# Two-layer attention and expert block: attention and queries on column halves of the array, maxima from high parts on row halves

## The reference

```python
q_hk = (hidden_q @ Wq.T).reshape(Bv, Sv, H, K)            # 16 heads, K = 128
q_big = einsum('bshk,hkq->bshq', q_hk, w_kc_q)            # q = 192
q_big = apply_rope(q_big, sin_q, cos_q)
kv_r = apply_rope(kv_c, sin_k, cos_k)                     # 1444 keys of 64
q_r = einsum('bshq,hqr->bhsr', q_big, W_qr)
k_r = einsum('bld,hdr->bhlr', kv_r, W_kr)
scores = einsum('bhsr,bhlr->bhsl', q_r, k_r)
attn = softmax(scores, axis=-1)
ctx_c = einsum('bhsl,bld->bhsd', attn, kv_r)
ctx_lat = einsum('bhsd,hkd->bhsk', ctx_c, w_kc_kv)
out = ctx @ Wo.T
```

## Time and profile before

| | |
|---|---|
| median of three runs | 2293.81 us |
| profiled execution, its own time | 2283.25 us |
| its span, first to last instruction | 2281.4 us |
| mean granted TensorE clock | 0.905 |
| TensorE matmul (PE) busy | 1857.9 us, 81% |
| VectorE (DVE) busy | 1492.1 us, 65% |
| ScalarE (ACT) busy | 1220.5 us, 53% |
| GpSimd (POOL) busy | 1117.1 us, 49% |

### The profile page before, as it was taken

The page is one execution under the profiler, slowest core; times in us unless marked ns, Lnnn a source line. Parts: engine busy times, 40 slices in busy tenths (PEclk is TensorE's granted clock), DMA queues, the critical chain, the costliest instruction groups (busy, mean ns, idle before and its releaser), DMA issues. The chain is left out here.

```text
span 2281.4 us, 38538 instructions
## 1 busy us (share of the span) xinstructions
PE 1857.9 (81%) x10550; PEld 1632.6 (72%) x10550; DVE 1492.1 (65%) x2799; ACT 1220.5 (53%) x2996; POOL 1117.1 (49%) x961
## 2 busy tenths in 40 slices
PE   4999958999999999999999973499993689837870
PEld 3677736888888888888888963499993466626870
DVE  4677777777777777767776433377774466656763
ACT  2111115777777767767777851366661266515650
POOL 0455528888788888878888852300004100014005
PEclk9999967999999999999999985699996599958985
DMA  5522251111111111111110002455542100026654
GB/s 159 197 58 57 55 176 55 63 63 63 45 54 63 64 31 63 63 64 63 63 54 11 16 8 78 140 197 196 204 165 58 34 1 0 0 77 196 198 164 113
DMA packets 115748, 195.76 MB, mean 86 GB/s; under 512 B 48213, under 2 KB 94265, under 8 KB 110161
## 3 DMA queue, kind: packets, MB, share of 16 engines
q1 hardware_dynamic: 107409, 180.88, 24.6%
q0 software_dynamic: 8192, 13.15, 2.0%
HBM read 147.01 MB, written 46.63 MB: 85 GB/s over the span
## 5 line engine op out<-in xcount | busy, mean ns | idle before, releaser
L501 POOL TENSOR_TENSOR EL<-E,EH 128x400 fp32r<-128x400 f32 x688 | 833.4, 1239 | 158.5 <-ACT EH L733 154.0
L599 DVE TENSOR_REDUCE PM<-bank 128x1 f32<-128x482 f32 (+1 forms) x624 | 397.2, 650 | 185.9 <-PE bank L578 182.9
L742 ACT ACTIVATE E<-bank 128x400 f32<-128x400 f32 x768 | 386.4, 503 | 212.8 <-PE bank L793 153.2
L733 ACT ACTIVATE EH<-E 128x400 fp32r<-128x400 f32 x768 | 407.0, 532 | 0.0
L175 PE MATMUL bank<-EH,KVH 128*128 128x400 f32 x768 | 283.1, 369 | 19.8 <-POOL EL L501 18.5
L578 PE MATMUL bank<-KH,QS 128*128 128x482 f32 (+1 forms) x624 | 250.9, 414 | 53.9 <-DVE KVL L549 27.6
L1248 POOL DMA_INDIRECT m_back<-rows_out,m_slots x64 | 64.8, 1013 | 450.8 <-DMA rows_out<-m_ys 421.2
L792 PE MATMUL bank<-QS,KH 128*128 128x400 f32 x768 | 272.1, 354 | 14.9 <-issue 9.1
L793 PE MATMUL bank<-QB,KB 66*128 66x400 f32 x768 | 269.1, 350 | 0.0
L175 PE MATMUL bank<-EH,KVL 128*128 128x400 f32 x768 | 265.7, 346 | 0.0
L175 PE MATMUL bank<-EL,KVH 128*128 128x400 f32 x768 | 265.5, 346 | 0.0
(11 more groups left out here) (244 smaller groups left out, 3983.3 us busy)
## 6 DMA issues: line engine op xcount, KB each, us to landing
m_stage_u<-in_m_up SPq DMA_DIRECT2D x20, 1392.0 KB
raw<-in_ctx_T SPq DMA_DIRECT2D x16, 1444.0 KB, 6.1
m_xg<-rows_in SPq DMA_DIRECT2D x55, 256.0 KB, 4.1
rows_out<-m_ys SPq DMA_DIRECT2D x55, 256.0 KB, 3.7
m_stage_d<-in_m_down SPq DMA_DIRECT2D x20, 696.0 KB
queries<-q_out SPq DMA_DIRECT2D x64, 200.0 KB, 2.4
QS<-queries SPq DMA_DIRECT2D x16, 800.0 KB, 6.1
rows_in<-zeros SPq DMA_DIRECT2D x5, 1792.0 KB
```

The source lines that it names most:

```text
L501: ops.tensor_tensor(EL[:, n % PB, :], E[:, n % EB, :], as_f32(EH[:, n % PB, :]), ALU.subtract).then_inc(sem, 1)
L599: nc.vector.tensor_reduce(PM[:, f:f + 1], psum[F0 + f % f_banks(b)][:, 0:KW[f % KC]], AX.X, ALU.max).then_inc(red_done, 1)
L733: nc.scalar.activation(EH[:, n % PB, :], E[:, n % EB, :], ACT.Copy).then_inc(hi_done, 1)
L742: nc.scalar.activation(E[:, n % EB, :], psum[S0 + n % SB][:, 0:CH], ACT.Exp).then_inc(exp_done, 1)
```

## The change

**Folding.** The 64 latent columns of `M2` are made once, not twice.

**Queries.** `narrow` works on a pair of heads: head 2j gives output rows 0 to 63, head 2j+1 rows 64 to 127 of one bank, four fp32 products of 64 columns of weights. The copy and the subtraction cover both heads at once, and SP stores a pair by four DMAs of 64 rows.

**Attention.** A step covers eight heads, so there are 24. `scores` has four products, even heads in one bank and odd heads in the next, with 128 rows in both kinds; one exponential of 2 x 400 columns reads both banks. `values` is two plain fp32 products, `KV` against the exponentials themselves, even heads to output rows 0 to 63 and odd heads to 64 to 127 of one bank; no high and low parts are made. The sums over keys are formed apart: VectorE sums the even heads' exponentials four key tiles at a time (`sum_even`), GpSimd adds the odd heads' tile by tile (`sum_odd`), and `sums` makes the sum over the 128 rows with a matrix of ones, again on two halves. The divisors take one DMA more each way.

**Maxima.** A piece uses the high parts of the queries alone, 64 rows: even pieces on rows 0 to 63 (from `QS`), odd ones on rows 64 to 127 (from `QB`, whose high queries now lie there). Two pieces follow each step's scores, and wait together for the two reductions before.

**Keys.** GpSimd rotates the keys, in ten parts; VectorE makes the last two, and the low and high copies of the key rows for `values` are gone. The fills of constant rows at the start are more, and the first query loads wait for them.

```diff
                 for half in range(2):
-                    nc.tensor.matmul(psum[2 + h % 2][0:HALF, half * P:(half + 1) * P],
-                                     wqr[:, h, half * HALF:(half + 1) * HALF],
-                                     wkr[:, h, :].rearrange("p (o d) -> p o d", o=1).to_broadcast([R0, 2, DC]),
-                                     start=True, stop=True)
...
+                        for row, part in enumerate((out_h, out_l)):
+                            for o in range(2):
+                                sp.dma_start(queries[bass.ts(c, CB)].rearrange("b p h s -> p h b s")[row * DC:(row + 1) * DC, 2 * j + o],
+                                             as_f32(part[o * DC:(o + 1) * DC, j % SLOTS, :]).rearrange("p (b s) -> p b s", b=CB)
+                                             ).then_inc(sent[j % SLOTS], 16)
                 for s in sent:
...
+                    pe.wait_ge(rot_done, c * H + (BUFS + 2 * j + 2))
+                    pe.wait_ge(lo_done, c * HP + (j + 1))
                     for half in range(2):
-                        last = nc.tensor.matmul(psum[4 + h % 2][:, 0:CH], M2[:, half, h, :], rot[:, h % TURNS, half, :],
-                                                start=half == 0, stop=half == 1)
+                        for o in range(2):
+                            h = 2 * j + o
+                            last = nc.tensor.matmul(psum[4 + j % 2][o * DC:(o + 1) * DC, 0:CH], M2[:, half, h, :],
+                                                    rot[:, h % TURNS, half, :], start=half == 0, stop=half == 1)
...
+                        if h >= 3 and h % 2:
+                            narrow(c, h // 2 - 1)
+                    narrow(c, HP - 1)
...
+                    v.wait_ge(hi_done, c * HP + (j + 1))
+
+                    nc.vector.tensor_tensor(out_l[:, j % SLOTS, :], psum[4 + j % 2][:, 0:CH],
+                                            as_f32(out_h[:, j % SLOTS, :]), ALU.subtract).then_inc(lo_done, 1)
 
...
+    HP = H // 4
     QT = -(-H * S // P)
     QW = QT * P
+    NS = 2 * KT
...
+    SB, FB = 2, 2
+    GT = 4
+    EB = 2 * GT
+    NG = NS // GT
+    EP = 2
...
+    S0, F0, CTX, MISC = 0, 4, 6, 7
+    SUM_AT, SUM0_AT, OUT_AT, TURN_AT = 2, 7, 8, 10
+    RECIP_AT, CT_AT = 9, 14
+    ROT_AT = (3, 4, 5, 6, 8, 9, 10, 11, 13, 14)
+    HI_AT, LO_AT = (17, 18), (18, 20)
+    ROT = 11
+    ADDS = KT - 1
     with ExitStack() as ctx:
...
+        def max_pieces(pe, b, pieces):
 
             r = b_mod(b)
-            t, j = divmod(f, KC)
-            banks = f_banks(b)
-            if f >= banks:
-                pe.wait_ge(red_done, b_val(b) * NF + (f - banks + 1))
+            depth = 2 * FB if b is FIRST else FB
+            if pieces[0] >= depth:
+                pe.wait_ge(red_done, b_val(b) * NF + (pieces[-1] - depth + 1))
             elif b is not FIRST:
                 pe.wait_ge(red_done, b_val(b) * NF)
-            nc.tensor.matmul(psum[F0 + f % banks][:, 0:KW[j]], QS[r][:, t * P:(t + 1) * P],
-                             KH[r][:, sum(KW[:j]):sum(KW[:j + 1])], start=True, stop=True).then_inc(f_ready, 1)
+            for f in pieces:
+                t, j = divmod(f, KC)
+                rows = slice((f % 2) * DC, (f % 2 + 1) * DC)
+                queries_of = QB if f % 2 else QS
+                nc.tensor.matmul(psum[f_bank(b, f)][:, 0:KW[j]], queries_of[r][rows, t * P:(t + 1) * P],
+                                 KH[r][rows, sum(KW[:j]):sum(KW[:j + 1])], start=True, stop=True).then_inc(f_ready, 1)
...
+        def sum_even(v, b, g, part):
+
+            cols = slice(part * (CH // 2), (part + 1) * (CH // 2))
+            p, q = divmod(g, KT // GT)
+            base = (g % 2) * (GT + 1)
+            if part == 0:
+                v.wait_ge(exp_done, b_val(b) * NS + ((g + 1) * GT + SB))
+            v.wait_ge(even_sum, b_val(b) * NG * 2 + (4 + 2 * g - 1 + part))
+            if q == 0:
+                src = R[:, base + 1:base + 1 + GT, 0, cols]
+            else:
+                src = R[:, base:base + 1 + GT, 0, cols]
+            if q == KT // GT - 1:
+                if part == 0 and b is not FIRST:
+                    v.wait_ge(sum_done, b_val(b) * 2 + (p - 1))
+                out = ES[:, p, 0, cols]
+            else:
+                out = R[:, ((g + 1) % 2) * (GT + 1), 0, cols]
+            nc.vector.tensor_reduce(out, src.rearrange("p t c -> p c t"), AX.X, ALU.add).then_inc(even_sum, 1)
+
+        def sum_odd(pool, b, n):
+
+            p, t = divmod(n, KT)
+            if t == 0:
+                return
+            pool.wait_ge(exp_done, b_val(b) * NS + (n + 1 + SB))
+            done = b_val(b) * 2 * ADDS + (p * ADDS + t - 1)
+            if t > 1 or p or b is not FIRST:
+                pool.wait_ge(odd_sum, done)
+            if t == KT - 1 and b is not FIRST:
+                pool.wait_ge(sum_done, b_val(b) * 2 + (p - 1))
+            first = R[:, slot(n - 1), 1, :] if t == 1 else EA[:]
+            out = ES[:, p, 1, :] if t == KT - 1 else EA[:]
+            nc.gpsimd.tensor_tensor(out, first, R[:, slot(n), 1, :], ALU.add).then_inc(odd_sum, 1)
+
+        def sums(pe, b, p):
+
+            pe.wait_ge(even_sum, b_val(b) * NG * 2 + (4 + NG * (p + 1)))
+            pe.wait_ge(odd_sum, b_val(b) * 2 * ADDS + ADDS * (p + 1))
+            if p == 0 and b is not FIRST:
+                pe.wait_ge(su_done, b_val(b) * 2)
+            for o in range(2):
+                last = nc.tensor.matmul(psum[MISC][o * DC:(o + 1) * DC, 0:CH], ones[:], ES[:, p, o, :], start=True, stop=True)
+            last.then_inc(sum_done, 1)
...
+                        act.wait_ge(av_done, b_val(b) * NS + (n + 1))
+                        if n % GT == 0:
+                            act.wait_ge(even_sum, b_val(b) * NG * 2 + (2 * (n // GT) + 2))
                         if n >= EB:
+                            act.wait_ge(odd_sum, odd_sums_to(b, n - EB))
                         elif b is not FIRST:
+                            act.wait_ge(odd_sum, odd_sums_to(before(b), NS + n - EB))
+                        k = S0 + 2 * (n % SB)
+                        nc.scalar.activation(R[:, slot(n), :, :], banks[:, k:k + 2, 0:CH], ACT.Exp).then_inc(exp_done, 1)
...
+                def scores(b, n):
+                    r = b_mod(b)
+                    p, t = divmod(n, KT)
+                    pe.wait_ge(exp_done, b_val(b) * NS + (n + 1))
+                    keys = slice(t * P, (t + 1) * P)
+                    for lhs, rhs in ((KH, QS), (KB, QB)):
+                        heads = rhs[r][:, p * 2 * CH:(p + 1) * 2 * CH].rearrange("p (j o s) -> p o j s", o=2, s=S)
+                        for o in range(2):
+                            last = nc.tensor.matmul(psum[S0 + 2 * (n % SB) + o][:, 0:CH].rearrange("p (j s) -> p j s", s=S),
+                                                    lhs[r][:, keys], heads[:, o], start=lhs is KH, stop=lhs is KB)
+                    last.then_inc(s_ready, 1)
                 def values(b, n):
 
-                    g, t = divmod(n, KT)
-                    wait_low(pe, b, n)
+                    p, t = divmod(n, KT)
+                    pe.wait_ge(exp_done, b_val(b) * NS + (n + 1 + SB))
                     if t == 0:
-                        pe.wait_ge(cu_done, b_val(b) * QG + (g + 1))
-                    cols = slice(t * KS, t * KS + P)
-                    split_products(nc, psum[A0 + g % 2][:, 0:CH],
-                                   [(KVH[b_mod(b)][:, cols], KVL[b_mod(b)][:, cols], EH[:, n % PB, :], EL[:, n % PB, :])],
-                                   first=t == 0, last=t == KT - 1).then_inc(av_done, 1)
+                        pe.wait_ge(cu_done, b_val(b) * 2 + (p + 1))
+                    for o in range(2):
+                        last = nc.tensor.matmul(psum[CTX][o * DC:(o + 1) * DC, 0:CH], KV[b_mod(b)][:, t, :], R[:, slot(n), o, :],
+                                                start=t == 0, stop=t == KT - 1)
+                    last.then_inc(av_done, 1)
 
                 def step(b, has_next, has_keys):
-                    r = b_mod(b)
                     pe.wait_ge(m_in, b_val(b) * 32 + 32)
-                    for n in range(NS):
-                        g, t = divmod(n, KT)
-                        pe.wait_ge(exp_done, b_val(b) * NS + (n + 1))
-                        out = psum[S0 + n % SB][:, 0:CH]
-                        keys, cols = slice(t * P, (t + 1) * P), slice(g * CH, (g + 1) * CH)
-                        nc.tensor.matmul(out, KH[r][:, keys], QS[r][:, cols], start=True, stop=False)
-                        nc.tensor.matmul(out, KB[r][:, keys], QB[r][:, cols], start=False, stop=True).then_inc(s_ready, 1)
-                        if has_next and n == F_AT:
-                            pe.wait_ge(k_ready, b_val(b) + 2)
-                            pe.wait_ge(q_in[b_mod(b + 1)], (b + 1).turn * 32 + 32)
-                        if has_next and 0 <= n - F_AT < NF:
-                            max_piece(pe, b + 1, n - F_AT)
```

(56 more changed lines are left out.)

314 lines of the change are left out of this document (142 added, 172 removed).

## The result

The changed kernel takes **2396.59 us** (median of four runs, 2385.91 to 2401.84) against 2294.51 for the kernel before on the same chip: a ratio of 1.045, with a 95% interval of 1.040 to 1.050. It is 4.5% slower; I had forecast 2255 us and faster. The profiled execution took 2401.84 us with a span of 2400.0, the profiled one of before 2283.25. Of these 118.6 us between the two, the queries account for -21.8 (SyncE issues the attention's first key load at 286.05 us, before the change at 307.81), the start of the attention for +13.9, the sixteen batches for +112.2 (first score to the first layer norm behind them: 1132.8 us against 1020.6), and the later stages, which nobody touched, for +14.2.

What follows compares the result with a forecast made beforehand. TensorE was taken to bound, GpSimd hardly less. Attention -19, queries -21, folding -2, start of the attention +10 gave -32 us against 2283.25, so 2251; half of the median's 10.6 excess on top gave 2255 us, range 2110 to 2420.

Steps and rivals of the forecast that it cites:

- Values, 1.67 us for four (bounds 1.33 and 2.67): Attention: four value products on two column halves take 1.67 us; wholly side by side 1.33, one after the other 2.67.
- Full overlap: Rival: value products wholly side by side, 1.33 us, batch 56.4, kernel 2174 us; chance 0.26 together with free shape changes.
- the staggered reading: Forecast case: issue order makes the second half start one record (0.33 us) late, five slots for four products; chance 0.51.
- Changes of shape: TensorE: each change of array shape costs 0.16 us, bounds 0 and 0.3, five times in two steps.
- Start of the attention +10: VectorE's new fills come to 21 us against 8.5 replaced, with one subtraction and some waits gone: 10 us more.
- 60.5 us against 61.7: Attention: a batch falls from 61.7 to 60.5 us; times 16 batches, 19 us less.
- 0.2 for the rows of maxima: End of a batch: waiting for the rows of maxima costs 0.2 us, with cover about as long as the earlier 4.9 us.
- Twelve sums at 1.18 ns: VectorE, each batch: twelve sums of 800 or 1000 elements at 1.18 ns an element, 13.2 us.
- hidden, barely: VectorE: a sum between two reductions makes 5.3 us, against the next pair's arrival at 4.8 + 0.42, so costs nothing.
- The new divisors' DMAs have seven steps of cover.: Attention: the two additional DMAs for the divisors have seven steps of cover.
- Halves that don't overlap: Rival: value products run one after the other, 2.67 us, batch 76 us, kernel 2526 us; chance 0.18.
- The clock: Rival: granted clock falls from 2.4 to 1.2 GHz through the attention, +45 us a batch, about 2970 us; chance 0.05.

Runs made afterwards that it cites:

- GpSimd's fills: Changed kernel with rows first, remainder and division earlier, sums in quarters, pieces on 128 rows, second and third buffers' constants filled by GpSimd: 2219.8 us, 0.970 of before.
- Rows and remainder together: Changed kernel with rows of maxima sent ahead of the key loads and the remainder taken a step earlier: 2320.8 us, 1.010 of the kernel before.
- Quarters: Changed kernel with rows first, remainder a step earlier, reciprocals and division two steps earlier, even heads' sums in quarters of the columns: 2249.2 us, 0.980 of before.
- short sums: Changed kernel with the even heads' partial sums reading one tile instead of four or five, same instructions and places: 2284.1 us, 0.995 of the kernel before.

## Why the prediction was wrong

The terms as the prediction put them:

- **Values, 1.67 us for four (bounds 1.33 and 2.67).** Measured 1.33 more than side by side when put on one half, and 1.50 us with the change of shape against 1.83 forecast. The halves are not staggered: the eight records start in twos, the two of a pair 0.01 us apart or less. The trace doesn't tell which half a record belongs to, so why the order of issue does not stagger them stays open. *Full overlap* was right in this, and the staggered reading was wrong.
- **Changes of shape, 0.16 each.** Pair of pieces to the next score 0.41 us; about right, and a pair of steps came to 4.64 against 4.80.
- **Pieces, 1.7 us from pair to pair.** 1.80.
- **Queries -21, folding -2.** -21.8 in the profile, -23 us alone on the chip: right.
- **Start of the attention +10.** +13.9; the fills took 27 us (286.26 to 313.57), since fifteen of them wait 0.25 to 0.40 us, nearly all for nothing that the profile shows, which no row I used had shown in a run of short fills. GpSimd gives back 14.5: from first key load to first score it is 64.5 us in the changed kernel, 50.1 with GpSimd's fills and 50.6 before.
- **The base of "60.5 us against 61.7".** 61.7 is one batch of before; the mean of fourteen is 62.65. A batch of 60.5 would have given 15 us more than the -19 that I put down.
- **"0.2 for the rows of maxima ... and the cover will be about as long."** This step failed first: in place of 0.2 us TensorE waits 5.1 in each batch, and runs at the lower clock behind it. Steps were moved, and I did not follow the moved ones through VectorE's and SyncE's queues. Before, turning to product was 4.9 us; after, 10.7. Rows and remainder together: 5.6 us a batch.
- **"Twelve sums at 1.18 ns"; "hidden, barely".** This failed second. I took the rate of a reduction along neighbouring columns in PSUM for a reduction whose neighbours are 800 columns apart in SBUF: 1.91 to 1.98 us instead of 1.18 for 1000 elements. Even my own sum had no room (5.3 us of VectorE against an arrival at 5.22) and I called it hidden; with the measured length it is late by some 0.9, in every second pair of steps. Quarters: 3.3 us a batch; sums cut to one tile, in the changed order: 7.9.
- **"The new divisors' DMAs have seven steps of cover."** They had; the division itself was put where ScalarE's copy waits for it, and the reciprocals where the pieces do: 1.9 us a batch together.

5.6 + 1.9 + 3.3 = 10.8 us a batch take 71.62 to 60.82, and the forecast was 60.5. None of my rivals was this one. *Halves that don't overlap* (2526) carried 0.18 of my 0.33 for slower, the largest part, and was false; the upper end of the range, 2420, was set by it, so that the measured 2397 lies inside the range is luck. (Its 226 us add up to 229 from the 76 us a batch, which changes nothing.) *The clock* I had as a fall for the whole attention, or none. What came was a consequence of waits: 0.50 to 0.75 in the 6.7 us behind a batch's gap of 5 to 6 us, some 4 to 5 us a batch in stretched products, and 0.91 over the attention; with the order mended, the same products on the same half arrays are granted 0.99 to 1.00. It is no cause of its own, but part of what each wait costs.

The Trainium skill ("SBUF — State Buffer", Door 1: The DMA port swizzle) says that SBUF is read in lines of 16 bytes, and that an access that leaves the line of the one before pays for it. The sums' inner step is 3200 bytes, and 1.9 to 2.0 ns an element against 1.18 agrees. The short sums, whose 200 elements are neighbours, agree too: reductions of neighbours last 0.20 us for 39 elements (L592), 0.35 for 200 and 0.65 for 480, about 1 ns for each further element, and the spaced ones 1.04 for 500 and 1.93 for 1000, about 1.8 (estimates from these medians). But the short sums also reduce one element in place of five, and no run here changed the step alone, so the cause of the slower rate is argued and only its size is shown.

60.8 us a batch is still 4.4 us more than my case of full overlap (56.4), so that the period came out near 60.5 is luck as well. About 1.8 of these are ten pairs of steps at 4.64 us where that case has 4.46. In the quarters' kernel some 2.7 us a batch are waits other than the 0.39 of each pair (an estimate from the batches' rows: 1.2 for the even sums, 0.8 for pieces, 0.5 for the last reduction before the turning, 0.2 for the rows), where I had allowed 0.7. What is left, some 0.6 us, stays open.

## What to carry to other kernels

A change that shortens the busiest engine moves every other engine's work nearer to its due time: for each moved step, follow its input through each queue it passes, and price what stands in front of it, before pricing what was saved. When two engines hand work to each other in short steps, the length of the longest instruction between two hand-overs counts and not the sum; splitting each sum into two equal halves paid 3.3 us of 64 here without removing any work. And before believing a bound, add work to it: 15 us of extra matmuls a batch cost 3.8, which says more than any busy share.

## What the runs showed of the hardware

- Two fp32 products on the two 64-column halves ran wholly side by side: 1.33 us less for four products of 400 columns than on one half. Two on 64-row halves start within 0.01 us.
- Small transfers issued behind 1.8 MB of loads landed 4.3 us after the issue of the second, against 1.7 us before the change, where the loads had gone out 4 us ahead of the rows and not 1.2; sent ahead of them, and with the remainder earlier, the wait fell from 5.1 to below 1 us a batch (13.3 in all).
- A VectorE addition of 128x400 from SBUF is 0.56 us alone and 1.03 beside a GpSimd addition. The division of 128x800 is 0.98 us alone or when it starts ahead of GpSimd's instruction (which then takes 2.51 us in place of 1.73), and 1.79 when GpSimd starts first. Reductions kept their time: 0.65 us for 480 columns with GpSimd busy or idle.
- Behind waits of 4.8 to 6.1 us the granted clock was 0.50 to 0.75 for the next 6.7 us, and it had been 1.00 ahead of them.
- GpSimd fills constants as fast as VectorE: 1.48 against 1.45 us for 1664 columns, whether 1 row or 64.
- A VectorE reduction of 1000 elements that lie 3200 bytes apart took 1.9 to 2.0 us, of 480 neighbouring columns 0.57.
